# Ready made PSUM offsets and eviction counts for TensorE in the build stage of a graph network kernel

## The reference

```
src, dst, w = sorted edges and their weights
counts[d, s]  = number of edges s -> d        # layer 0: agg = counts @ (h * norm_src)
weights[d, s] = sum of w over edges s -> d    # layer 1: out = weights @ (h @ W), degrees from its row sums
```

## Time and profile before

| what | value |
|---|---|
| median of 3 runs | 3700.72 us |
| profiled execution, first to last instruction (its span; the page gives no other time of it) | 4103.0 us |
| instructions in the profile | 80080 |
| mean granted TensorE clock | 0.832 of 2.4 GHz |
| busy: TensorE matmuls | 3139.2 us (77%) |
| busy: VectorE | 1986.4 us (48%) |
| busy: ScalarE | 1606.3 us (39%) |
| busy: GpSimd | 1627.3 us (40%) |

### The profile page before, as it was taken

The page is one execution under the profiler, slowest core; times in us unless marked ns, Lnnn a source line. Parts: engine busy times, 40 slices in busy tenths (PEclk is TensorE's granted clock), DMA queues, the critical chain, the costliest instruction groups (busy, mean ns, idle before and its releaser), DMA issues. The chain is left out here.

```text
span 4103.0 us, 80080 instructions
## 1 busy us (share of the span) xinstructions
PE 3139.2 (77%) x17480; PEld 1972.5 (48%) x17480; DVE 1986.4 (48%) x6935; ACT 1606.3 (39%) x4621; POOL 1627.3 (40%) x1766
## 2 busy tenths in 40 slices
PE   3788788879997797577777777777866778787877
PEld 2444444444443343455566656556643444444445
DVE  6656666556656115344444444444673444444442
ACT  1555555413322001233333333333453444444445
POOL 2000000024333001666666666666106666666660
PEclk7899898999998998687777777877977888888885
DMA  1111111125557995322222222222112222222220
GB/s 38 57 59 57 57 59 59 51 93 193 188 177 261 406 360 185 65 54 55 54 55 54 55 54 53 54 55 54 40 28 56 66 63 66 64 66 63 66 61 13
DMA packets 417722, 370.64 MB, mean 90 GB/s; under 512 B 175608, under 2 KB 342232, under 8 KB 417336
## 3 DMA queue, kind: packets, MB, share of 16 engines
q1 hardware_dynamic: 365912, 315.65, 23.8%
q0 software_dynamic: 46144, 48.98, 6.5%
q10 hardware_dynamic: 5280, 1.23, 0.1%
HBM read 279.65 MB, written 86.00 MB: 89 GB/s over the span
## 5 line engine op out<-in xcount | busy, mean ns | idle before, releaser
L1451 POOL DMA_INDIRECT big<-row_table,src x806 | 761.5, 945 | 487.3 <-issue 183.4
L1870 POOL DMA_INDIRECT big<-message_table,src x610 | 612.0, 1003 | 394.5 <-DVE big L2000 172.1
L1476 PE MATMUL banks<-big 97*128 x902 | 399.8, 534 | 148.6 <-issue 138.1
L1492 PE MATMUL banks<-big 128*128 x1804 | 349.0, 326 | 174.8 <-ACT big L1508 110.1
L486 PE MATMUL banks<-work 128*128 128x226 f16 x1197 | 350.3, 293 | 138.6 <-issue 131.0
L1492 PEld LDWEIGHTS banks<-big 128*128 128x128 f32 x1804 | 312.4, 244 | 202.5 <-issue 202.1
L1909 PE MATMUL banks<-big 128*128 128x512 f16 x1225 | 395.6, 441 | 4.4 <-DVE big L1988 4.4
L850 PE MATMUL banks<-big,work 128*128 128x512 f16 (+1 forms) x1750 | 352.1, 359 | 22.3 <-DVE work L984 17.4
L1541 DVE TENSOR_REDUCE big<-banks 128x1 f32<-128x256 f32 x451 | 189.4, 420 | 332.5 <-PE banks L1476 183.8
L1508 ACT COPY big<-banks 128x256 f32<-128x256 f32 x451 | 169.8, 377 | 439.5 <-remote 194.0
L1918 PEld LDWEIGHTS banks<-big 128*64 128x64 f32 x1804 | 173.8, 164 | 343.6 <-issue 343.0
(11 more groups left out here) (338 smaller groups left out, 5835.8 us busy)
## 6 DMA issues: line engine op xcount, KB each, us to landing
big<-weights_halves SPq DMA_DIRECT2D x16, 6400.0 KB, 20.8
weights_dense<-work SPq DMA_DIRECT2D x196, 200.0 KB, 1.9
work<-weights_dense SPq DMA_DIRECT2D x196, 200.0 KB, 2.7
weights_halves<-work SPq DMA_DIRECT2D x98, 400.0 KB, 2.6
big<-q_table SPq DMA_DIRECT2D x451, 64.0 KB
big<-in_ef SPq DMA_DIRECT2D x403, 64.0 KB
big<-in_ea SPq DMA_DIRECT2D x403, 32.0 KB
big<-row_table,src POOLq DMA_INDIRECT x806
```

The lines of the kernel that those rows point to most:

```text
L1451: po.indirect_dma_start(rows[:, t % RT, s, 0:D], None, x_t.rearrange("a p c -> (a p) c"), bass.IndirectOffsetOnAxis(ap=m.src2[:, s, t:t + ...
L1476: pe.matmul(psS[v % 2], qT[v % R][0:XW, :], XF[0:XW, bass.ds(slot, 1), :].rearrange("p t e -> p (t e)"), start=False, stop=True).then_inc( ...
L1492: ins = pe.matmul(psA[v % 2], PT[v % 2][:, s * P:(s + 1) * P], rows[:, bass.ds(slot, 1), s, :].rearrange("p t c -> p (t c)"), start=(s == ...
L1870: po.indirect_dma_start(G[n % R][:, s, :], None, g_t.rearrange("a p c -> (a p) c"), bass.IndirectOffsetOnAxis(ap=m.src2[:, s, t:t + 1], ax ...
```

## The change

`stage_tables` no longer packs. It writes, as 32 bit words, for each visit its PSUM offset (bank times 512) and for each half batch the number of freed pairs to wait for (newest j halved, plus 1). Two batches make a *leg*: 20 offsets and 4 counts, 24 words; there are 60 legs, 20 in each of partitions 0, 32 and 64 of `work`, behind what the build uses of it. TensorE loads one leg at a time without range checks, uses the offsets directly, and only masks the count to 8 bits. The three matmuls of a visit, the waits and their order are the same, and no other engine of the build changes.

```diff
+LEG = 2 * TP
+NLEG = VT // LEG
+WALK = LEG + LEG // GV
+WALK_AT = 6160
...
+    def leg(self, g):
+        i, at = divmod(g, NLEG // 3)
+        return self.walk(i)[:, at * WALK:(at + 1) * WALK]
...
             chain(dve.tensor_copy(jI, valid))
+            chain(dve.tensor_scalar(pairI, jI, 1, None, ALU.arith_shift_right))
             chain(dve.tensor_scalar(jI, jI, BANKS - 1, None, ALU.bitwise_and))
-            chain(dve.tensor_copy(tmp, jI))
...
-            chain(dve.scalar_tensor_tensor(code, five[:, :, GV - 1], float(BANKS), five[:, :, GV - 2], ALU.mult, ALU.add))
-            for u in range(GV - 3, -1, -1):
-                chain(dve.scalar_tensor_tensor(code, code, float(BANKS), five[:, :, u], ALU.mult, ALU.add))
-            chain(dve.scalar_tensor_tensor(m.steps(), code, float(JMAX), newest, ALU.mult, ALU.add))
+            for i, row in enumerate(WALK_ROWS):
...
+                chain(dve.tensor_scalar(to[:, :, 0:LEG], part(jI).rearrange("p (g v) -> p g v", v=LEG), 512, None, ALU.mult))
+                newest = part(pairI).rearrange("p (g q u) -> p g q u", g=NLEG // 3, u=GV)[:, :, :, GV - 1]
+                chain(dve.tensor_scalar(to[:, :, LEG:WALK], newest, 1, None, ALU.add))
...
-            def codes(g, n):
-                _, xs = nc.values_load_multi_w_load_instructions(m.steps()[:, bass.ds(g, n)], [mybir.EngineType.PE], min_val=0,
-                                                                 max_val=JMAX * BANKS ** GV - 1)
...
+            def leg(g):
+                _, xs = nc.values_load_multi_w_load_instructions(m.leg(g), [mybir.EngineType.PE], min_val=0, max_val=(BANKS - 1) * 512,
+                                                                 skip_runtime_bounds_check_because=BOUNDED)
+                return xs[0:LEG], xs[LEG:WALK]
...
-                pe.wait_ge(freed, ((x & (JMAX - 1)) >> 1) + 1)
-                for u in range(n):
-                    t = GV * half + u
-                    bank = (x >> (JBITS + 3 * u)) & (BANKS - 1)
-                    to = lambda c0, c1: m.PS[:, bass.ds(bank, 1), c0:c1].rearrange("p b c -> p (b c)")
+                pe.wait_ge(oh_ready, b + 1)
+                for t in range(min(TP, V0 - b * TP)):
+                    if t % GV == 0:
+                        pe.wait_ge(freed, needed[t // GV] & 255)
+                    to = lambda c0, c1: flat[:, bass.ds(places[t] + c0, c1 - c0)]
...
+            for g in range(NLEG):
+                places, needed = leg(g)
+                for u in range(2):
+                    batch(2 * g + u, places[u * TP:(u + 1) * TP], needed[u * (TP // GV):(u + 1) * (TP // GV)])
```

More of the change, by code:

```diff
@@ L46 @@
 GV = 5
-NG5 = -(-V0 // GV)
 VT = NBATCH * TP
+LEG = 2 * TP
+NLEG = VT // LEG
+WALK = LEG + LEG // GV
+WALK_AT = 6160
+BOUNDED = "the table is written from values that are clamped when it is made"
 CW = NCH * BB
@@ L51 @@
 BANKS = 8
-JBITS = 9
-JMAX = 1 << JBITS
 ROW, COL, CHUNK, WHI, WLO = range(5)
@@ L66 @@
 NDC = -(-NDST // DC)
-BLOCK1, ENDS, BLOCK2 = 0, 32, 96
+ENDS, BLOCK2 = 32, 96
+WALK_ROWS = (0, 32, 64)
 R = 8
@@ L136, in __init__, with walk @@
         self.landed_q = [sem(f"landed_q{i}") for i in range(R)]
-    def steps(self):
-        return self.vis[BLOCK1:BLOCK1 + 1, :].bitcast(I32)[:, 0:NG5]
+    def walk(self, i):
+        row = WALK_ROWS[i]
+        return self.work[row:row + 1, WALK_AT:WALK_AT + NLEG // 3 * WALK].bitcast(I32)
+    def leg(self, g):
+        i, at = divmod(g, NLEG // 3)
+        return self.walk(i)[:, at * WALK:(at + 1) * WALK]
     def ends(self):
@@ L197, in stage_tables @@
         cmpJ = take(C0 * J0 // 2).bitcast(BF16).rearrange("p (c j) -> p c j", c=C0)
-        ends, steps = take(J0), take(NG5)
+        ends = take(J0)
         r1 = take(K1 * 3 * TB).bitcast(I32).rearrange("p (k a e) -> p k a e", k=K1, a=3)
@@ L329, in _ @@
             chain(dve.tensor_scalar(valid, j1, float(J0 - 1), None, ALU.min))
+            pairI = tmp.bitcast(I32)
             chain(dve.tensor_copy(jI, valid))
+            chain(dve.tensor_scalar(pairI, jI, 1, None, ALU.arith_shift_right))
             chain(dve.tensor_scalar(jI, jI, BANKS - 1, None, ALU.bitwise_and))
-            chain(dve.tensor_copy(tmp, jI))
-            five = tmp[BLOCK1:BLOCK1 + 1, 0:GV * NG5].rearrange("p (k u) -> p k u", u=GV)
-            newest = valid[BLOCK1:BLOCK1 + 1, 0:GV * NG5].rearrange("p (k u) -> p k u", u=GV)[:, :, GV - 1]
-            code = steps[BLOCK1:BLOCK1 + 1, :]
-            chain(dve.scalar_tensor_tensor(code, five[:, :, GV - 1], float(BANKS), five[:, :, GV - 2], ALU.mult, ALU.add))
-            for u in range(GV - 3, -1, -1):
-                chain(dve.scalar_tensor_tensor(code, code, float(BANKS), five[:, :, u], ALU.mult, ALU.add))
-            chain(dve.scalar_tensor_tensor(m.steps(), code, float(JMAX), newest, ALU.mult, ALU.add))
+            n = VT // 3
+            for i, row in enumerate(WALK_ROWS):
+                to = m.walk(i).rearrange("p (g w) -> p g w", w=WALK)
+                part = lambda v: v[row:row + 1, i * n:(i + 1) * n]
+                chain(dve.tensor_scalar(to[:, :, 0:LEG], part(jI).rearrange("p (g v) -> p g v", v=LEG), 512, None, ALU.mult))
+                newest = part(pairI).rearrange("p (g q u) -> p g q u", g=NLEG // 3, u=GV)[:, :, :, GV - 1]
+                chain(dve.tensor_scalar(to[:, :, LEG:WALK], newest, 1, None, ALU.add))
             dve.wait_ge(s_tv, 3)
@@ L470, in _, with batch @@
         def _(pe):
-            def codes(g, n):
-                _, xs = nc.values_load_multi_w_load_instructions(m.steps()[:, bass.ds(g, n)], [mybir.EngineType.PE], min_val=0,
-                                                                 max_val=JMAX * BANKS ** GV - 1)
[L474 to L480, removed]
-                pe.wait_ge(freed, ((x & (JMAX - 1)) >> 1) + 1)
-                for u in range(n):
-                    t = GV * half + u
-                    bank = (x >> (JBITS + 3 * u)) & (BANKS - 1)
-                    to = lambda c0, c1: m.PS[:, bass.ds(bank, 1), c0:c1].rearrange("p b c -> p (b c)")
+            flat = m.PS[:, :, :].rearrange("p b c -> p (b c)")
+            def leg(g):
+                _, xs = nc.values_load_multi_w_load_instructions(m.leg(g), [mybir.EngineType.PE], min_val=0, max_val=(BANKS - 1) * 512,
+                                                                 skip_runtime_bounds_check_because=BOUNDED)
+                return xs[0:LEG], xs[LEG:WALK]
+            def batch(b, places, needed):
+                rows, cols = slots[b % 2]
+                pe.wait_ge(oh_ready, b + 1)
[3 more added lines that the diff above has]
+                    to = lambda c0, c1: flat[:, bass.ds(places[t] + c0, c1 - c0)]
                     pe.matmul(to(CW, CW + CAW), rows[:, 0, t, :], cols[:, t, :], start=False, stop=True, skip_group_check=True)
```

## The result

The kernel after the change takes 3461.43 us (median of 4 runs, 3460.03 to 3463.11) against 3700.72 us before: a ratio of 0.935, with a 95% interval of 0.9339 to 0.9361, or 239.3 us less.

A forecast was written before the change was run, and what follows sets the result against it. TensorE's instruction stream, held by register instructions, was taken as the build's bound. Less assumed recording cost, the build would fall from 537 to 430 us, a gain of 107 from 3700.72: forecast 3595 us, range 3475 to 3668.

The forecast's parts named there:

- Term (a): TensorE's stream in the build: shift and mask gone from 1197 visits, address operation one step shorter; gain 218 us.
- Term (c): TensorE's stream in the build: range checks on 240 loaded words go; gain 68 us.
- Term (e): Table stage on VectorE: changed operations hide behind a 12.03 us wait for row transfers; cost nothing.
- rival 2: Build: ScalarE becomes the bound, 3660 us, chance 0.11; second half: clock sinks to 1.2 GHz in some batches, 3663, chance 0.04.
- From the profile to the runs: Whole kernel: 402.3 us of span over median is recording cost; build before 537 us unrecorded, after 430, gain 107 us.
- The recorded sum: Build stage as profiled: falls from 702 to 435 us, the span from 4103 to some 3836 us.
- rival 1: The build carries little of the recording excess, so recorded numbers hold: gain 160 to 265 us, 3436 to 3540; chance 0.18.
- (d), the load: TensorE's table loads: 60 of 24 words at 0.74 us replace 30 of 8; net cost 28 us, other bound 1.77 us each.
- Rival 3: TensorE's 24 word load: above 3.05 us the kernel gets slower; at 269 ns a word 3901 us; chance 0.03.
- What is late next: Build after the change: VectorE sets the pace at 3.55 us a batch, ScalarE level; with 2% added, 435 us.

## Why the prediction was wrong

**What held.** The bound before was TensorE's own stream, with VectorE and ScalarE at slack. Term (a): 218 us forecast, 231 measured. It also had the fused address operation shrink by one of four steps: no run shows the number of steps, and what the runs show is the length of its record, a median of 60 ns before, 46 after and 55 with the shift and the mask put back. Term (c): 68 forecast, 67 measured. Term (e), the table's making, was put at nothing: the first load starts at 85.9 and, in its second profile, at 84.0 us, against 83.2 before. The kernel before itself starts its visits at 87.3 us in one profile and at 89.2 in the other, so there is nothing to be seen that exceeds this scatter. The forecast of the visits at 0.265 us was right (0.24 to 0.27), and the granted clock stays at 0.99, where the second half of rival 2 had it sinking.

**The step that failed: "From the profile to the runs".** I had a span of 4103.0 us and a median of 3700.72, and made the difference a cost of recording, which I then spread over register instructions. The recorded sum gave 702 to 435 us, a gain of 267. On this ground 165 us were struck off the build before the change (537 us) and 5 off the one after it (430), so that 107 were left. The runs show an execution's time and its span 1.8 us apart: 4117.28 and 4115.5 us for the kernel before, 3460.91 and 3459.1 for the kernel after. The 402 us are a difference between executions at two levels, which nothing on record but the chip and the time of the run sets apart, and they lie in attention and the messages. For the same code, the granted clock there, the length of the stretch and the records of one line:

```profile
1664.00:3006.00 1342.00, 991.18 (x5286) 802.46 (x5286) 601.70 (x3141) 515.14 (x1749) 754.72 (x800) 0.78 0.25 53
```

```profile
L1476 PEldq ALU_OP  x1691: 4/36/839, 1664.3 to 3006.7; - x188
```

These are of the kernel before on the chip where it took 4110.7 us, and these of the kernel after on the chip where before took 3708.58 us:

```profile
1414.00:2508.00 1094.00, 876.09 (x5290) 706.02 (x5290) 617.08 (x3145) 526.54 (x1752) 755.68 (x800) 0.90 0.31 65
```

```profile
L1486 PEldq ALU_OP  x1691: 32/36/48, 1414.4 to 2507.6; - x188
```

GpSimd's gathers are as long on both (754.7 and 755.7 us busy), but on the slower chip single register instructions of this line last up to 839 ns, where the other has none above 48. They are a sign of the level and not the sum of it: all register records of TensorE in the attention add up to 258 us there and to 200 here, 58 of the 249 us by which the stage differs. The earlier trace rows showed this already: a median of 36 ns with a longest of 839 is no even stretch of every instruction by 25 or 36 ns, as I had made it. Taken seriously, that row says that the build, whose ALU_OPs are 36/36/36, has none of the excess, and that is rival 1: "the recorded numbers hold", 3436 to 3540 us, for which I gave 0.18. Its time came, 3461 us, but its reason only in half: the late stages do hold the excess, and recording has no part in it. Nor did the range allow for it: 3475 cut off the part of rival 1 in which the result lies. I had argued against it that the late stages are full of register instructions too; the answer was in the longest durations of the earlier trace rows.

**The term that was mis-sized: (d), the load.** Forecast 0.74 us, from the slope between a load of 2 words and one of 8, with 1.77 us named as the other bound; measured 1.84 us, just above that bound. By the rule above the 2 word load pays 0.27 us for each word and the 8 word load 0.30 us for each four, so that their slope of 9 ns a word was an accident. The net cost of the loads is 60 x 1.93 less 30 x 0.65, 96 us and not 28. Rival 3, slower through a dear load, had the point of decision at 3.05 us from a build of 537 us that was never there. But the price it named, 269 ns a word, is the real one of an unaligned table: with the table 8 bytes further on, the kernel is 1.5% slower than before. That the kernel after was faster at all was luck in this respect: it hung on an address to which neither the change nor the prediction gave a thought.

**What is late next.** I had VectorE, with TensorE's stream at 3.1 us a batch. Two batches take 454.1 / 60 = 7.57 us. Less the 17 us of waits, TensorE's stream itself needs (454.1 - 17) / 60 = 7.28 us with its load of 1.84, against 2 x 3.53 = 7.06 us on VectorE, so the stream stayed the bound, by a little. The timeline of VectorE shows both: batches 3.52 us apart, where it waits for nothing, and longer where it waits for the matmuls behind a load.

```profile
299.45 0.83 DVE L457 TENSOR_TENSOR work<-iotaH,work 128x1280 f16<-128x1280 f16 x1 [0.29 <-PE banks L498]
...
302.97 0.82 DVE L457 TENSOR_TENSOR work<-iotaH,work 128x1280 f16<-128x1280 f16 x1
...
307.13 0.83 DVE L457 TENSOR_TENSOR work<-iotaH,work 128x1280 f16<-128x1280 f16 x1 [0.55 <-PE banks L498]
```

As the two paths differ by 3%, the miss cost little: the visits were forecast at 435 us in a profile and took 454. By the recorded sum alone, 702 to 435, the kernel would have been put at 3434 us, 27 us too low; how much of that is the load, no run shows by itself. So the last step did the harm, and without it the forecast would have been within 1%, mis-sized term and all.

## What to carry to other kernels

Where a profile's span and the times of the runs differ by a tenth, find out first whether they come from the same chip, by comparing a recorded execution's own time with its span (1.8 us apart here); don't explain the gap by a cost of recording, and look at the longest duration of a group of records before stretching all of them. On an engine whose own stream is the bound, count register instructions by the distance between starts (0.1 us each here), not by their records (36 ns), and have the words ready made, unchecked, and at a multiple of 16 bytes (a load of 24 words took 1.84 us there and 6.17 us at 8 bytes behind one). A coarser wait saves instructions and can cost more than it saves: with one wait in ten visits in place of five, the kernel here was 20 us slower.

## What the runs showed of the hardware

- **The price of a register load goes by where it starts.** From a multiple of 16 bytes four words take about 0.30 us; from 8 bytes behind one, each word takes about 0.26 us. 24 words: 1.84 or 6.17 us, 22 words: 2.10 or 5.70 us. ScalarE's load of four words takes 0.310 us.
- **Span and time of one execution agree.** They differ by 1.8 us in both kernels, before and after, and at both levels.
- **The same kernel has different levels on different chips.** It took 3708.58, 4110.7 and 4135.1 us on three chips, each used at one time only, where runs on one chip mostly agree within 0.3% (one of the 15 on the first took 4164.04 us). The layers took 874.6 us on the first slow chip and 873.1 on the fast one; attention and messages, whose code is the same in both kernels, took 1348.4 and 996.9 us there against 1099.0 and 840.9, which is 249 and 156 us. On the slow chip single ALU_OPs of TensorE last up to 0.84 us in the attention and 1.4 us in the messages. What holds them, and where the larger part of the difference comes from, was not found out.
- **A division or a remainder added 47 ns** to the sequencer's fused address operation (46 to 93 ns).
- **GpSimd's copy took up to 3.59 us, as long as a chain of VectorE's operations.** The copy of L439 (before: L429) took 35.23 us for 118, 299 ns each, and 94.45 us for 118, 800 ns, after, for the same copy. In the timeline one takes 0.27 us when VectorE is idle, and 3.58 us when it starts 0.15 us behind VectorE's L457 (302.97 us, above), until 306.70, 0.13 us behind the end of the batch's last operation. A busy VectorE alone does not do it: with 12 words a load it is as busy (434 of 454 us), and the copies took 61.2 us, none over 0.96 us, so the moment at which a copy starts counts. VectorE waited 7.8 us for GpSimd in the visits. What makes the copy long, no run tested.

```profile
299.22 0.27 POOL L439 COPY work<-work 128x100 f16<-128x100 f16 x1 [2.79 <-DVE work L462]
...
303.12 3.58 POOL L439 COPY work<-work 128x100 f16<-128x100 f16 x1 [3.63 <-DVE work L462]
```
